# Attention queries in two halves of 512, and a freed PSUM bank that projects batch 0 inside head groups 5 and 6

## What is computed

```
q = LN(x) @ Wq                       # 16 heads of 16
k, v = split(concat(ctx, LN(x)) @ Wkv)   # 154 + 1024 keys
dots = q k^T / 4, masked where j > i + 154
x = x + softmax(dots) v @ Wout + bout
x = x + FFN(LN(x))     # 8 experts, top-256 tokens of each expert, then
                       # every token goes to one expert: gate * gelu(x W1[e]) W2[e]
```

## Time and profile before

| | us |
|---|---|
| median of 3 runs (lowest to highest) | 391.06 (390.84 to 391.16) |
| profiled execution, its own time | 390.64 |
| its span, first to last instruction | 388.8 |
| attention: first to last exponential | 75.7 to 245.6 |
| tail, up to the second means2 | 245.6 to 266.0 |

### The profile page before, as it was taken

How to read it: one execution, slowest core, us unless ns; L and a number is a source line. 1 busy time by engine, 2 the same in 40 slices (tenths; PEclk the granted TensorE clock), 3 DMA queues, 4 the chain that set the end, 5 groups by cost and what they waited for, 6 DMA issues and landing times.

```text
span 388.8 us, 10940 instructions
## 1 busy us (share of the span) xinstructions
PE 355.1 (91%) x4322; PEld 230.0 (59%) x4322; DVE 210.2 (54%) x730; ACT 266.0 (68%) x386; POOL 114.7 (29%) x157
## 2 busy tenths in 40 slices
PE   8879899999999999999999999992886899999993
PEld 7647454644444435354535444581775799999993
DVE  4948748844465546373645456398777523232330
ACT  2455555599999999999999999424732264545530
POOL 5234755400003030110203022400440735555522
PEclk9999999999999999999999999998565999999998
DMA  8433886340256716454448424504430322222100
GB/s 264 128 117 101 269 237 192 121 168 3 75 135 218 176 42 164 146 155 119 113 138 247 123 45 135 174 2 167 158 110 2 103 82 93 76 97 92 61 28 29
DMA packets 37037, 47.68 MB, mean 123 GB/s; under 512 B 8732, under 2 KB 26066, under 8 KB 36977
## 3 DMA queue, kind: packets, MB, share of 16 engines
q1 hardware_dynamic: 34080, 40.26, 35.1%
q0 software_dynamic: 2560, 6.30, 5.3%
q10 hardware_dynamic: 337, 0.32, 0.2%
HBM read 32.71 MB, written 13.81 MB: 120 GB/s over the span
## 4 chain that ended last, share of the span: by engine, by line
PE 69%; DVE 12%; ACT 12%; issue 3%; DMA 2%; POOL 1%; SPq 0%; POOLq 0%; DVEq 0%; ACTq 0%
PE ps L1096 18%; PE ps L1075 16%; PE ps L1276 9%; ACT pbuf L834 9%; PE ps L1288 8%; PE ps L1060 8%; PE ps L1013 5%; DVE v_st L1712 2%; DMA pbuf<-in_L_xattn_Wkv 2%; DVE pbuf L1584 2%; DVE stats L1618 1%; DVE xe L1613 1%; PE ps L1265 1%; PE ps L1158 1%; ACT mid L795 1%
## 5 line engine op out<-in xcount | busy, mean ns | idle before, releaser
L834 ACT ACTIVATE pbuf<-ps 128x1024 f32<-128x1024 f32 (+3 forms) x192 | 168.9, 1032 | 2.1 <-PE ps L1075 2.1
L1584 DVE SCALAR_TENSOR_TENSOR pbuf<-pbuf,seen 128x128 f32<-128x128 f32 (+2 forms) x288 | 74.9, 300 | 63.7 <-ACT pbuf L834 62.8
L1075 PE MATMUL ps<-q_st,k_st 98*32 98x512 bf16 (+4 forms) x2048 | 101.4, 318 | 2.6 <-ACT pbuf L834 2.5
L1096 PE MATMUL ps<-pbuf,v_st 128*32 128x512 f32 (+4 forms) x1024 | 96.8, 473 | 2.2 <-DVE pbuf L1584 2.1
L1075 PEld LDWEIGHTS ps<-q_st,k_st 98*32 98x32 bf16 x2048 | 51.9, 96 | 68.2 <-issue 26.7
L702 POOL TENSOR_TENSOR mid<-mid 64x1024 f32<-64x1024 f32 x7 | 16.6, 2373 | 121.3 <-DMA mid<-reciprocals 121.3
L1096 PEld LDWEIGHTS ps<-pbuf,v_st 128*32 128x32 f32 x1024 | 27.4, 109 | 27.5 <-issue 11.5
L1276 PEld LDWEIGHTS ps<-mid,piece_f 128*128 128x128 f32 x320 | 38.8, 192 | 2.1 <-issue 1.2
L1276 PE MATMUL ps<-mid,piece_f 128*128 128x128 f32 x320 | 39.3, 275 | 0.8 <-issue 0.8
L1288 PE MATMUL ps<-pbuf,mid 128*128 128x256 f32 x160 | 37.7, 379 | 0.0
L1060 PE MATMUL ps<-mid,pbuf 128*128 128x512 f32 (+1 forms) x80 | 32.5, 542 | 5.2 <-ACT mid L795 4.1
(11 more groups left out here) (252 smaller groups left out, 380.3 us busy)
## 6 DMA issues: line engine op xcount, KB each, us to landing
wts<-in_L_ffn_W SPq DMA_DIRECT2D x16, 512.0 KB, 4.8
k_st<-k_cut SPq DMA_DIRECT2D x48, 147.2 KB, 3.0
q_st<-q_cut SPq DMA_DIRECT2D x48, 128.0 KB, 2.9
q_cut<-wts SPq DMA_DIRECT2D x8, 384.0 KB, 3.1
k_cut<-wts SPq DMA_DIRECT2D x8, 384.0 KB, 4.0
xe<-in_x SPq DMA_DIRECT2D x4, 512.0 KB, 6.9
token_rows<-xe SPq DMA_DIRECT2D x4, 512.0 KB, 4.1
mid<-mid SPq DMA_DIRECT2D x28, 64.0 KB, 2.5
```

Source lines behind the costliest of these rows:

```text
L834: nc.scalar.activation(pbuf[:, s % 2, r, c0:c1], st_ps[(s * GH + r) % NST][:, c0:c1], ACT.Exp, scale=SCALE).then_inc(exp_done, 1)
L1075: last = nc.tensor.matmul(st_ps[(s * GH + r) % NST][c:c + 32, a:z], k_st[pa][:, r, t * P + c:t * P + c + 32], q_st[pa][:, r, q0 + a - c0:q ...
L1096: last = nc.tensor.matmul(o_ps[32 * r:32 * r + 32, a:z], v_st[pa][:, t, r, :], pbuf[:, s % 2, r, a + dc:z + dc], start=(t == 0), stop=(t = ...
L1584: last = nc.vector.scalar_tensor_tensor(a, a, 3.0e38, seen[:, off:off + w], ALU.min, ALU.mult)
```

## The change

Each group now treats queries 0 to 511 and then 512 to 1023. `half_steps` makes two steps of the lower half (tiles 0, 1; tiles 2, 5, 3, 4, 872 columns) and four of the upper (tiles 0, 1; 2, 3; 4, 5; 6, 9, 7, 8, 872 columns): six steps and 5840 columns as before, and as many matmuls in the same sizes. `o_ps` is one bank. Masked are steps 0, 1, 4 and 5; steps 2 and 3 are not. Two whole diagonal blocks 512 columns apart are masked by one instruction. The copy of `o_ps` is made twice in a group, 512 columns each: take_outputs(g, 0) at step 2, and take_outputs(g, 1) in step 0 of group g + 1, between the masks of its heads 1 and 2.

The other bank (bank 7, `side_ps`) projects batch 0: `side_row` in groups 5 and 6 at steps 0, 1, 3 and 4, one row of 128 tokens each, before the second half of the values; VectorE adds the row and takes its statistics in the same step. In group 7, step 3, the lower half of the last group is flipped in bank 7, in step 4 turned back, and ScalarE takes it in step 5. After the last group eight rows and one half are left. SyncE's queue sends the pack ahead of the stage. VectorE computes the reciprocals at step 3, where they stood at step 4 before (in group 7 at step 3 as before).

```diff
-STEP_TILES = [[0], [5, 6], [4, 7], [3, 8, 9], [1], [2]]
...
+HALF = S // 2
+def half_steps(lo, hi):
+    whole = [t for t in range(JT) if first_query(t) <= lo]
+    part = [t for t in range(JT) if lo < first_query(t) < hi]
+    steps = [[[(t, lo, HALF * i)] for i, t in enumerate(whole[n:n + 2])] for n in range(0, len(whole), 2)]
+    a, b, c, d = [(t, first_query(t), hi - first_query(t)) for t in part]
+    steps.append([[(a[0], a[1], 0), (d[0], d[1], a[2])], [(b[0], b[1], HALF), (c[0], c[1], HALF + b[2])]])
...
+STEPS = half_steps(0, HALF) + half_steps(HALF, S)
...
+UPPER_STEP = [s for s in range(NSTEP) if STEPS[s][0]][0]
...
+MASKED = [s for s in range(NSTEP) if diagonals(s)]
...
+FLIP_AT = (LAST, UPPER_STEP + 1)
+BACK_AT = (LAST, UPPER_STEP + 2)
+TAKE_AT = (LAST, UPPER_STEP + 3)
+ROW_AT = [(g, s) for g in (2 * KT + 1, 2 * KT + 2) for s in (0, 1, 3, 4)]
...
-        o_ps = ps[:, 1024 * NST:1024 * NST + 1024]
+        o_ps = ps[:, 1024 * NST:1024 * NST + HALF]
+        side_ps = ps[:, 1024 * NST + HALF:1024 * NST + 2 * HALF]
...
                 sums_away(g)
+                pack(g)
                 if g + 2 < 2 * NG:
                     stage(g % 2, (g + 2) // NG, (g + 2) % NG // 2, range(0, NPROD // 2))
                 sums_back(g)
-                pack(g)
...
             def values(pa, s, g0, half):
...
+                if lo == pieces[0][0][1] and pieces[0][0][0] == 0 and half == 0:
+                    pe.wait_ge(raw_done, 2 * g0 + (1 if lo else 0))
+                if s in MASKED:
+                    pe.wait_ge(mask_done, (g0 * len(MASKED) + MASKED.index(s) + 1) * GH)
+                else:
                     pe.wait_ge(exp_done, (g0 * NSTEP + s) * GH + GH + NST)
...
                     scores(pa, s, NST, g0)
+                    if (g0, s) in ROW_AT:
+                        side_row(ROW_AT.index((g0, s)))
+                    elif (g0, s) == FLIP_AT:
+                        pe.wait_ge(raw_done, 2 * LAST + 1)
+                        pe.wait_ge(x1_done, QT)
+                        flip(0)
+                    elif (g0, s) == BACK_AT:
+                        back(0)
                     values_before(1, pa, s, g0, before_g)
+
+            def side_row(n):
+                pe.wait_ge(scaled, NG)
+                pe.wait_ge(extra_done, 2)
+                if n:
+                    pe.wait_ge(x1_done, n)
+                at = n * P
+                for k in range(KT):
+                    for c in range(0, P, 32):
+                        last = nc.tensor.matmul(side_ps[c:c + 32, 0:D + E], pk[:, 0, k, at + c:at + c + 32], wout_sb[:, k, :],
+                                                start=(k == 0), stop=(k == KT - 1), skip_group_check=True)
+                last.then_inc(wo_ready, 1)
...
+                values(1, NSTEP - 1, LAST, half)
+            pe.wait_ge(scaled, LAST)
             pe.wait_ge(back_done, 1)
...
+            wout(8)
+            wout(9)
+            pe.wait_ge(last_raw, 1)
+            flip(1)
+            wout(10)
+            wout(11)
+            back(1)
+            pe.wait_ge(back_done, 2)
+            for n in range(12, TT):
                 pe.wait_ge(x1_done, n - 3)
...
+            def masks(g0):
+                for s in range(NSTEP):
...
+                    if g0 > 0 and s == UPPER_STEP + 1:
+                        reciprocals(g0 - 1)
+                    if s == UPPER_STEP:
+                        take_outputs(g0, 0)
...
+                    for r in range(GH):
+                        if s in MASKED:
+                            v.wait_ge(exp_done, (g0 * NSTEP + s) * GH + r + 1 + NST)
+                            last = mask(pbuf[:, s % 2, r, :], diagonals(s))
+                            last.then_inc(mask_done, 1)
+                        if r == 1 and g0 and s == 0:
+                            take_outputs(g0 - 1, 1)
+                    if (g0, s) == FLIP_AT:
+                        divide(0)
+                    if (g0, s) in ROW_AT:
+                        n = ROW_AT.index((g0, s))
+                        x1_row(n)
+                        stats2(n)
+                        if n == QT - 1:
+                            means2(0, QT)
...
+            def take_outputs(g0, half):
+                if half == 0:
+                    v.wait_ge(biased, TT // 2)
+                    if g0:
+                        v.wait_ge(sums_out, 16 * g0)
+                        v.wait_ge(packed, 16 * GH * g0)
+                v.wait_ge(pv_done, g0 * NSTEP + (NSTEP if half else UPPER_STEP) + 2)
+                nc.vector.tensor_copy(raw[:, HALF * half:HALF * (half + 1)], o_ps).then_inc(raw_done, 1)
...
+            x1_row(8)
+            x1_row(9)
+            stats2(8)
+            stats2(9)
+            divide(1)
+            refine2(0, 0, QT, True)
+            x1_row(10)
+            x1_row(11)
```

More of the change, by code:

```diff
@@ L1071, in scores @@
                 pe.wait_ge(exp_done, (g0 * NSTEP + s) * GH + r + 1)
[L1072 to L1078 removed]
+                hi = STEPS[s][1]
@@ L1079, in scores @@
+                for (t, q0, c0) in sum(STEPS[s][3], []):
+                    for c in range(0, P, 32):
+                        last = nc.tensor.matmul(st_ps[(s * GH + r) % NST][c:c + 32, c0:c0 + hi - q0],
+                                                k_st[pa][:, r, t * P + c:t * P + c + 32],
+                                                q_st[pa][:, r, q0:hi], start=True, stop=True, skip_group_check=True)
                 last.then_inc(st_ready, 1)
             def values(pa, s, g0, half):
-                pieces = VALUE_PIECES[s][half]
@@ L1091, in values @@
                     pe.wait_ge(exp_done, (g0 * NSTEP + s) * GH + GH + NST)
-                else:
-                    pe.wait_ge(mask_done, g0 * ((NSTEP - 1) * GH) + s * GH)
-                for (t, a, z, dc) in pieces:
+                for (t, q0, c0) in pieces[half]:
                     for r in range(GH):
-                        last = nc.tensor.matmul(o_ps[32 * r:32 * r + 32, a:z], v_st[pa][:, t, r, :],
-                                                pbuf[:, s % 2, r, a + dc:z + dc],
-                                                start=(t == 0), stop=(t == STEP_TILES[-1][-1]), skip_group_check=True)
+                        last = nc.tensor.matmul(o_ps[32 * r:32 * r + 32, q0 - lo:hi - lo], v_st[pa][:, t, r, :],
+                                                pbuf[:, s % 2, r, c0:c0 + hi - q0],
+                                                start=(t == 0), stop=(w < HALF and half == 1), skip_group_check=True)
@@ L1099, in values @@
                 if half == 1:
                     last.then_inc(pv_done, 1)
-                elif g0 == LAST and s == NSTEP - 1:
-                    last.then_inc(pv_upper, 1)
             def maxima(pa, g0):
@@ new lines, in mask @@
+            def mask(row, at):
+                cols = row.rearrange("p (k n) -> p k n", k=2)
+                if [m[1:] for m in at[:2]] == [(P, 0), (P, 0)]:
+                    (c0, w, off), (c1, _, _) = at[:2]
+                    assert c1 == c0 + HALF
+                    a = cols[:, :, c0:c0 + w]
+                    last = nc.vector.scalar_tensor_tensor(a, a, 3.0e38, seen[:, None, :].broadcast_to([P, 2, P]), ALU.min, ALU.mult)
+                    at = at[2:]
+                for (c0, w, off) in at:
+                    a = row[:, c0:c0 + w]
+                    last = nc.vector.scalar_tensor_tensor(a, a, 3.0e38, seen[:, off:off + w], ALU.min, ALU.mult)
+                return last
@@ new lines, in take_outputs, with group @@
+            def take_outputs(g0, half):
[6 more added lines that the diff above has]
+                nc.vector.tensor_copy(raw[:, HALF * half:HALF * (half + 1)], o_ps).then_inc(raw_done, 1)
+            def group(pa, g0, fl):
+                with v.If(fl > 0):
+                    take_maxima(pa, g0)
+                masks(g0)
@@ L1670, in _ @@
+            seq(nc.vector.memset(mx, -3.0e38))
+            v.wait_ge(flag_done, 2)
+            for g in range(2 * NG):
+                if g % (2 * KT) == 0:
+                    fl = v.value_load(flag[0:1, g // (2 * KT):g // (2 * KT) + 1], min_val=0, max_val=1)
+                group(g % 2, g, fl)
             x1_row(8)
-            means2(0, QT)
+            x1_row(9)
             stats2(8)
-            x1_row(9)
+            stats2(9)
+            divide(1)
             refine2(0, 0, QT, True)
-            stats2(9)
@@ L1676, in _ @@
-            for n in range(10, TT):
+            x1_row(10)
+            x1_row(11)
+            stats2(10)
+            stats2(11)
+            for n in range(12, TT):
                 x1_row(n)
```

200 lines of the change are left out of this document (51 added, 149 removed).

## The result

| | before | after |
|---|---|---|
| median, us (4 runs each) | 391.11 (390.84 to 392.30) | 404.69 (403.18 to 406.27) |
| profiled execution; its span | 390.64; 388.8 | 403.18; 401.4 |
| attention, first to last exponential | 75.7 to 245.6 (169.9) | 75.8 to 266.5 (190.7) |
| first wout behind attention to the start of the last means2 | 18.14 | 10.17 |

The ratio, worked out over the single runs and so not quite the quotient of the medians, is 1.036, 95% interval 1.0337 to 1.0384. 396.5 was forecast, with a range up to 400.0: the direction was right and the size was not. Attention grew by 20.8 us and the tail gave 8.0 back.

A forecast was written before the change was run, and what follows sets the result against it. ScalarE was taken to set attention's pace at 21.1 us a group, TensorE nearly full beside it. 5.8 + 2.1 + 1.5 + 2.5 + 0.3 - 6.8 = +5.4 us gave 396.0 profiled, median 396.5; 8-in-10 range 390.6 to 400.0.

The forecast's parts named there:

- (d): Groups 2, 3, 4, 6, 7: masks meeting GpSimd's scale cost 0.6 us each, +2.5 us net; ends -1.2 and 7.0.
- (b): Group 5, step 0: the first side row waits for scale(3), stalling TensorE; +2.1 us, ends 0 and 3.1.
- the halving itself: All groups: columns, matmul sizes and exponentials stay, second copy covered; 0 us, upper end 1 us per group.
- (a): Groups 5 and 6: eight side rows at 0.91 us, less TensorE's slack; +5.8 us, ends 4.1 and 6.9.
- (c): Group 7: early flip and back on TensorE plus take_back on ScalarE; +1.5 us, ends 0.5 and 2.6.
- (e): End of attention: the last step's masks are three instructions per head in place of one; +0.3 us.
- (f): Tail: fewer rows and one half left behind attention, 18.1 us becomes 11.35; gain 6.8 us, ends 6.3 and 7.3.
- Rival B: Attention takes the rows in, with TensorE slack of 1.6 us a group; -3.1 us, 387.9 us; chance 0.20.
- Rival C: Terms at bad ends together, as scale wanders through steps meeting masks repeatedly; +13.6 us, 404.6 us; chance 0.07.
- that of (b): Group 5: TensorE idle 2 us before the first side row, ended by GpSimd's scale.
- that of (d): Step 0 masks of 1 to 2.3 us beside scale, groups 3 and 4 over 21.5 us; all at 0.3 refutes.
- that of (f): Tail: first wout behind attention to last means2 takes 11.3 us in place of 18.1.

The follow-up runs named there:

- late_scale: late_rows, with GpSimd's scale also held to steps 2 and 3, which have no masks: 391.57 us, ratio 1.0020.
- scale_in_step0: late_scale with scale held only until the previous group's last values, so it starts on step 0's masks: 405.27 us, ratio 1.0334.
- before_scale_on_masks: Kernel before the change, with scale held until step 0's values are done, so it meets step 2's masks: 402.69 us, ratio 1.0288.
- late_rows: Changed kernel with the eight side rows moved to later places in groups 5 to 7: 402.61 us, ratio 1.0283.
- filled_wait: Changed kernel with 30 unused matmuls on TensorE ahead of the first side row's wait in group 5: 402.32 us, ratio 1.0268.
- first_places: Changed kernel with its own side row places, scale held to steps 2 and 3 for every scale but scale(3): 396.74 us, ratio 1.0146.
- late_scale_no_rows: no_rows with scale held to steps 2 and 3, as in late_scale: 393.25 us, ratio 1.0025.
- late_scale_places: late_scale with the side rows at other steps, two of them moved from step 1: 391.62 us, ratio 1.0002.
- no_rows: Changed kernel with all sixteen projections behind attention; halves and early flip stay: 399.88 us, ratio 1.0234.
- take_later: late_scale_filled with late_scale_places' row steps, and the upper half's copy behind head 2's mask instead of head 1's: 389.90 us, ratio 0.9975.
- late_scale_filled: late_scale with 6 unused matmuls behind each of the first three scores of group 0: 390.87 us, ratio 0.9991.

## Why the prediction was off, step by step

The steps that failed are three of nearly the same size: the price of a meeting in (d), 2.2 us short; the wait in (b), 2.5 us short, with the clock's fall behind it; and the halving itself, which stood at nothing and cost 2.6. The theory that the experiments began with, that meetings are most of what was under-forecast, does not hold for this sum; the wait of late_scale takes away meetings that the forecast had counted, too.

Together, in the profiled executions: 5.9 (a) + 4.6 (b) + 1.8 (c) + 4.7 (d) + 0.3 (e) - 8.0 (f) + 2.6 and 1.1, two terms that the prediction didn't have, - 0.6 behind the tail, is +12.4 us. The span grew by 12.5, against 5.4 forecast. (The median of after lies 1.5 us above its profiled execution.) The steps:

**(d), masks against GpSimd, failed as a price: 0.6 us for every meeting, where it is anything from 0.26 to 1.96 and 1.2 in the mean.** The places were right (groups 2, 3, 4, 6, 7; scale began just ahead of the last two). Against plain groups of 21.33 without a meeting, the five cost 1.6, 0.26, 0.45, 1.96 and 1.86 (the side rows and the flip taken off at their own prices): 6.1 us, less 1.4 for the two meetings that the time before had in it, 4.7 net against 2.5. The price was read from two groups in which scale reached few masks that TensorE needed at once. What it lacked is the moment: scale begins 0.7 and 0.9 us into groups 3 and 4, where TensorE still has other work while a mask stands, and 3.0 us into group 2, where it has none. There a meeting is a stall of the value matmuls, which stand in order ahead of the scores that feed ScalarE, so 1.4 to 2.1 us of TensorE's idle time come out as idle time of the engine that sets the pace. The bound of 1.5 us, "when one mask waits for all of L702", was passed by three of the five. late_scale, scale_in_step0 and before_scale_on_masks show this cause by moving nothing but scale: -11.0, +13.7 and +11.3 us. These are more than the 4.7, because they hold the clock's falls behind meetings (one in before_scale_on_masks, two each in late_rows and scale_in_step0) and six meetings in place of five.

The rule of the Trainium skill ("SBUF — State Buffer", section "Who interferes with whom") named the mechanism, and the traces after agree: masks with pbuf and seen as inputs stood until scale was done (0.42 became 2.46 us), and the copy out of PSUM beside it kept its 0.69. It gave no price, and the price is in the pipeline behind.

**(b), the first side row's wait: 2.1 forecast, 4.6 measured** (28.89 less a plain group and four rows at 0.74). That scale(3) would come nearer to the group's start, since a half copy is over sooner, didn't happen: it began 2.8 us into group 5 against 2.7 before, and TensorE stood 3.04 us, at the upper end of what the term allowed. What no term had is the clock: behind the wait it was granted at 0.56 and 0.59 for two stretches of 2 us. filled_wait, with TensorE kept busy, takes 1.8 us off group 5; first_places, where the clock stayed up, has 2.6 us for a wait of 2.35. So about 1.8 of the 4.6 are the clock and 2.8 the wait. The remark that everything queued behind would wait was right.

**(a), the side rows: 5.8 forecast, 5.9 measured** by late_scale against late_scale_no_rows (four rows in a group are 2.96 us, and after has two such groups). The number is partly luck. The split, 0.91 us a row less 0.75 us of slack once in each group, would give 0.16 us for a single row in a group and 1.07 for two; one row cost 0.59 (late_scale, group 5: 21.92) and two cost 1.27 (late_scale_places, group 5: 22.60). The price goes by the row and by its step, with no slack that the first one uses up. Rival B's slack of 1.6 us isn't there either.

**(c), group 7: 1.5 forecast, 1.8 measured**, from two errors that cancelled: the row of 1.04 us in the earlier trace rows has eight matmuls, both halves, so a half's flip is 0.6, and of flip and back 1.05 us were paid, with hardly any slack to hide in; and step 5 grew by 0.71, take_back's 0.58 us on ScalarE in full and perhaps some of the last meeting.

**(f), the tail: -6.8 forecast, -8.0 measured**, mostly by the same misreading: flip and back at 0.60 in place of 1.04 are 0.9 of the 1.2 us. **(e)**: 0.3 and 0.3.

**Not in the sum at all: the halving itself, 2.6 us.** "Columns, matmul sizes and number of exponentials stay", so it was put at 0. In late_scale_no_rows a plain group is 21.33 against 21.07 to 21.10, and group 0, where its clock doesn't fall, is 21.84 (no_rows) against 20.99: 7 x 0.25 + 0.85. In the plain groups the loss sits at the ends of the two steps of 872 columns. From the start of head 3's exponential to that of the next one are 1037 to 1046 ns in step 1 and 1120 to 1134 in step 5, where the others of these steps are 778 apart: 0.26 and 0.35 us. Before, the same two steps lost 0.16 to 0.18 and 0.15 (1002 to 1017 against 841 ns, 966 against 819). The exponentials themselves aren't slow there: they take 927 to 972 ns in step 1 and 1012 to 1046 in the wider step 0 (each begins before the last one's end in the trace, so the distances are shorter). take_later tried one cause, the second copy's place, and the 0.26 stayed: **why the next exponential starts late is open.** That TensorE's round is too long beside the short exponentials of a narrow step would look like this, and no run tested it. The other term is group 0's clock, 0.50 from 80 to 83 us, 1.1 us in the profiled execution of after; late_scale_filled shows that it goes when TensorE is kept busy through the first scores.

**Rival C**, all terms at their bad ends, had a chance of 0.07 and gave 404.6, which is nearly the time, by luck in part. Its mechanism was half right: scale did wander through the steps and met masks again and again. But (a), (c), (d) and (f) weren't at their bad ends; (b), which went beyond its own, and two terms that it hadn't made up for them. Of the signs listed, that of (b) was asked for at 2 us (3.04 came), that of (d) at groups 3 and 4 over 21.5 (21.59 and 21.78; without the 0.25 of the halving group 3 would have missed it), that of (f) at 11.3 (10.17).

## What to carry to other kernels

When a change moves the steps of a pipeline, list the instructions of the helper engines that keep their own time (here one of 2.4 us on GpSimd, once a group), and see which work of the others they will now stand beside: a stop costs what waits behind it in order, not the length of the stopped instruction, and the same stop cost 0.12 or 1.6 us by where in the group it fell. Hold such an instruction to a place without conflicts with a wait that costs nothing; here that gave back 11 of the 12 us that the rearranged kernel of late_rows had lost, and no more: with it the rearrangement is level with the kernel before (ratio 1.0020). And read the count in a row (x8 or x4) before its time is taken for one piece.

## What the runs showed of the hardware

TensorE's granted clock fell from 1.00 to near 0.50 (1.2 GHz) inside attention, which before kept 1.00 in groups 2, 4 and 7. It fell behind idle time of 3.04 us (after, group 5), of 2.1 and 2.0 us (late_rows, groups 6 and 7), of 1.70 us (before_scale_on_masks, group 5) and of 1.45 us (scale_in_step0, group 4); it did not fall behind 2.35 us in first_places, behind 2.09 us in after (group 7), nor behind the same 1.70 us in the other groups of before_scale_on_masks. So the length of the idle stretch just ahead doesn't tell alone; what else does, is open. A fall costs 1.7 to 1.8 us of a group (24.50 against 22.82; 28.89 against 27.07), as much as the meeting in front of it.

A side row, 16 float32 matmuls in the trace, in four 32-wide tiles side by side, took 1.06 to 1.10 us at full clock as merged in the timeline, and lengthened its group by 0.74 in the mean. A row of the tail with the same output, four 128-wide matmuls in the trace, took 0.91 before and 0.96 after (3.83 us for four rows).

Masks (VectorE, two inputs in SBUF) that began beside scale (GpSimd) stood until it was done, up to 2.47 us in place of 0.42 (late_rows) and 2.03 in place of 0.27 (late_scale_no_rows); copies out of PSUM beside it kept 0.69 us, and scale its 2.34 to 2.47.
